# The statistics pass of a two-layer graph network: a sixth selected chunk, one absolute on VectorE, five difference buffers, pair squares one instruction later

## The reference, cut to what matters

```
D = |x[b,i] - x[b,j]|                       for every pair i, j of rows of a batch
h = W1 D + b1                               (64 values per pair)
m, v = mean and variance of h over ALL batches and pairs, per channel
s = W2 . leaky((h - m) / sqrt(v + eps) * g1 + be1) + b2
A = softmax of s over j, where A_init allows the pair
y = A x, a linear layer, batch norm, leaky; out = layernorm(x + [x, y] Wt + bt)
```

## Time and profile before

| what | us |
|---|---|
| median of three runs | 2326.1 (2325.75 to 2334.32) |
| the profiled execution, its own time | 2333.18 |
| its span, first to last instruction | 2330.9 |
| PE (TensorE matmul) busy | 1995.3, 86% |
| DVE (VectorE) busy | 2120.4, 91% |
| ACT (ScalarE) busy | 2165.3, 93% |
| POOL (GpSimd) busy | 43.2, 2% |

### The profile page before, as it was taken

The page is one execution under the profiler, slowest core; times in us unless marked ns, Lnnn a source line. Parts: engine busy times, 40 slices in busy tenths (PEclk is TensorE's granted clock), DMA queues, the critical chain, the costliest instruction groups (busy, mean ns, idle before and its releaser), DMA issues.

```text
span 2330.9 us, 35023 instructions
## 1 busy us (share of the span) xinstructions
PE 1995.3 (86%) x12741; PEld 799.4 (34%) x12741; DVE 2120.4 (91%) x2647; ACT 2165.3 (93%) x2988; POOL 43.2 (2%) x50
## 2 busy tenths in 40 slices
PE   5777777899999898989889899996899999999976
PEld 4555553333333333333333333332222222222226
DVE  5888868999999999999999999998999999999966
ACT  5999987999999999999999999996999999999975
POOL 0000000000000000000000000000000000000000
PEclk8999988999999999999999999998999999999997
DMA  4111104444444444444444444443899989989962
GB/s 122 42 42 42 42 15 149 183 182 180 190 182 181 185 181 184 186 184 177 185 174 185 180 180 190 176 186 156 341 349 354 354 347 357 352 340 354 352 242 73
DMA packets 221280, 470.49 MB, mean 202 GB/s; under 512 B 52344, under 2 KB 143288, under 8 KB 196536
## 3 DMA queue, kind: packets, MB, share of 16 engines
q1 hardware_dynamic: 220048, 467.91, 53.1%
q10 hardware_dynamic: 1064, 0.36, 0.1%
HBM read 254.25 MB, written 213.91 MB: 201 GB/s over the span
## 4 chain that ended last, share of the span: by engine, by line
ACT 42%; issue 23%; PE 13%; DMA 10%; DVE 9%; SPq 4%; ACTq 0%; POOLq 0%; POOL 0%; DVEq 0%
ACT hcopy L625 8%; ACT habs L625 8%; ACT yt L630 8%; ACT diff L613 7%; DMA ring_scores<-sring 4%; DVE ring L1085 4%; ACT habs L657 3%; PE banks L784 3%; PE banks L870 3%; PE banks L955 2%; DMA hcopy<-kept 2%; DMA diff<-kept 2%; ACT banks L635 2%; PE banks L794 2%; SPq L453 2%
## 5 line engine op out<-in xcount | busy, mean ns | idle before, releaser
L870 PE MATMUL banks<-diff,w1t 128*64 128x512 f32 x5136 | 1207.8, 603 | 122.0 <-ACT hcopy L625 57.0
L1213 DVE TENSOR_TENSOR diff<-ring 128x2048 f32<-128x2048 f32 x352 | 802.4, 2287 | 42.1 <-PE banks L870 42.1
L870 PEld LDWEIGHTS banks<-diff,w1t 128*64 128x64 f32 x5136 | 346.7, 137 | 855.3 <-issue 808.3
L1227 DVE TENSOR_SCALAR diff<-diff 128x2048 int32<-128x2048 int32 x354 | 418.2, 1220 | 0.0
L1353 DVE TENSOR_TENSOR diff<-ring 128x2048 f32<-128x2048 f32 x128 | 292.5, 2285 | 17.6 <-PE banks L870 17.4
L613 ACT ACTIVATE diff<-banks 128x2048 f32<-128x2048 f32 x128 | 238.5, 1863 | 2.8 <-PE banks L885 2.8
L955 PE MATMUL banks<-habs,w2s 128*32 128x512 f32 x816 | 159.1, 600 | 55.0 <-ACT hcopy L657 22.4
L630 ACT ACTIVATE yt<-hcopy,par 128x2048 f32<-128x2048 f32 x96 | 192.5, 2005 | 3.1
L630 ACT ACTIVATE yt<-habs,par 128x2048 f32<-128x2048 f32 x96 | 192.4, 2005 | 3.1
L625 ACT ACTIVATE hcopy<-banks 128x1024 f32<-128x1024 f32 x192 | 193.8, 1018 | 0.6 <-PE banks L870 0.6
L625 ACT ACTIVATE habs<-banks 128x1024 f32<-128x1024 f32 x192 | 193.7, 1018 | 0.3 <-PE banks L870 0.3
(11 more groups left out here) (215 smaller groups left out, 1929.0 us busy)
## 6 DMA issues: line engine op xcount, KB each, us to landing
kept<-hcopy SPq DMA_DIRECT2D x192, 512.0 KB, 2.9
kept<-habs SPq DMA_DIRECT2D x192, 512.0 KB, 2.9
hcopy<-kept SPq DMA_DIRECT2D x78, 1024.0 KB, 8.1
diff<-kept SPq DMA_DIRECT2D x76, 1024.0 KB, 8.3
habs<-kept SPq DMA_DIRECT2D x38, 1024.0 KB, 8.4
yt<-xrows SPq DMA_DIRECT2D x512, 40.0 KB, 2.0
adjt<-in_adj_dram SPq DMA_DIRECT2D x32, 256.0 KB, 2.8
diff<-in_x_dram SPq DMA_DIRECT2D x32, 128.0 KB, 2.1
```

What stands on the lines that cost most here:

```text
L870: last = nc.tensor.matmul(dst[half * O:(half + 1) * O, bank * BANK:(bank + 1) * BANK], w1t[:, :], src[:, m * BANK:(m + 1) * BANK], start=T ...
L1213: v.tensor_tensor(shaped(diff[:, c % ND, :]), xj, xi_, ALU.subtract).then_inc(sub_done, 1)
L1227: v.tensor_scalar(bits, bits, ABS_BITS, None, ALU.bitwise_and).then_inc(abs_dve, 1)
```

## The change

Five edits, all in the statistics pass but the last:

1. ORDER is changed, and (1, 1) joins the selected chunks: six of 16 instead of five. They stand at places 0, 3, 6, 8, 11 and 14.
2. The absolute of the selected chunk (0, 1), at place 8, is taken by VectorE out of `dps` (`absolute_of_picked`). ScalarE keeps five: four with a sum, one without, as before. VectorE has ten subtractions and ten absolutes in SBUF, before eleven of each.
3. ND is 5 instead of 4, and `band` gives up two of its three planes for the room. The build of the mask uses `prob` for a while, and GpSimd's masking reads the one plane twice.
4. The square of a pair of copies stands behind the next chunk's `sum_h` in ScalarE's queue and ahead of the absolute, no longer right behind the pair's second copy.
5. VectorE's order is written out anew, to fit.

The blocks of x for the selections grow with the number of selected chunks (NP = 6).

```diff
-    ND = 4
+    ND = 5
-    ORDER = [(0, 0), (4, 0), (4, 1), (1, 0), (5, 0), (5, 1), (2, 0), (6, 0), (6, 1), (3, 0), (7, 0), (7, 1),
-             (0, 1), (1, 1), (2, 1), (3, 1)]
-    ON_PE = [(0, 0), (1, 0), (2, 0), (3, 0), (0, 1)]
+    ORDER = [(0, 0), (4, 0), (4, 1), (1, 0), (5, 0), (5, 1), (2, 0), (2, 1), (0, 1), (6, 0), (6, 1), (3, 0),
+             (7, 0), (7, 1), (1, 1), (3, 1)]
+    ON_PE = [(0, 0), (1, 0), (2, 0), (0, 1), (3, 0), (1, 1)]
+    PE_TO_DVE = [(0, 1)]
...
-        band = sb("band", [P, 3, P])
+        band = sb("band", [P, P])
...
@@ ScalarE
-                    if n % 2:
-                        both = hcopy if n % KB < 4 else habs
-                        src = both[:, n % 4 - 1:n % 4 + 1, :].rearrange("p q n -> p (q n)")
-                        act.wait_ge(kept_copied, n + 1)
-                        nc.scalar.activation(spare, src, ACT.Square, bias=par[:, 53:54],
-                                             accum_out=column(SQUARES + B * NR + n // 2)).then_inc(sq_kept, 1)
...
+            def square_pair(n):
+                both = hcopy if n % KB < 4 else habs
+                src = both[:, n % 4 - 1:n % 4 + 1, :].rearrange("p q n -> p (q n)")
+                act.wait_ge(kept_copied, n + 1)
+                nc.scalar.activation(spare, src, ACT.Square, bias=par[:, 53:54],
+                                     accum_out=column(SQUARES + B * NR + n // 2)).then_inc(sq_kept, 1)
...
                 for j in range(CHUNKS):
                     sum_h(b, j)
-                    if j + 3 in PE_AT:
+                    if pair_ends_at(b, j - 1):
+                        square_pair(b * NK + kept_before(j - 1))
+                    if j == 0 and b:
+                        square_pair(b * NK - 1)
+                    if j + 3 in ACT_AT:
                         absolute(b, j + 3)
...
@@ TensorE, pick_differences
-                if n:
-                    pe.wait_ge(abs_pe, n)
-                e = 2 * pe_before(j)
+                last_pick = [i for i in PE_AT if i < j]
+                if last_pick and last_pick[-1] not in ACT_AT:
+                    pe.wait_ge(abs_dve, b * (CHUNKS - NA) + dve_before(last_pick[-1]) + 1)
+                elif n:
+                    pe.wait_ge(abs_pe, b * NA + act_before(j))
+                k, tp = ORDER[j]
+                e = 2 * (RECTS * tp + k)
...
@@ VectorE
+            def absolute_of_picked(b, j):
+                c = in_order(b, j)
+                dve.wait_ge(pd_ready, b * NP + pe_before(j) + 1)
+                dve.wait_ge(h_ready, c - ND + 1)
+                v.tensor_scalar(diff[:, c % ND, :].bitcast(I32), dps.bitcast(I32), ABS_BITS, None,
+                                ALU.bitwise_and).then_inc(abs_dve, 1)
...
-                    differences_between(b, 1, 3)
-                differences_between(b, 4, 6)
-                differences_between(b, 7, 9)
-                differences_between(b, 10, 12)
+                    subtract(b, 1)
+                    subtract(b, 2)
+                    absolute_at(b, 1)
+                    absolute_at(b, 2)
+                subtract(b, 4)
+                subtract(b, 5)
+                absolute_at(b, 4)
+                subtract(b, 7)
+                absolute_at(b, 5)
+                absolute_at(b, 7)
+                subtract(b, 9)
+                absolute_of_picked(b, 8)
+                subtract(b, 10)
+                absolute_at(b, 9)
+                absolute_at(b, 10)
+                subtract(b, 12)
+                absolute_at(b, 12)
                 subtract(b, 13)
-                subtract(b, 14)
+                subtract(b, 15)
                 absolute_at(b, 13)
-                subtract(b, 15)
-                absolute_at(b, 14)
                 absolute_at(b, 15)
```

More of the change, by code:

```diff
@@ L57, in gnn_pair_kernel @@
     PE_AT = [j for j, c in enumerate(ORDER) if c in ON_PE]
+    ACT_AT = [j for j in PE_AT if ORDER[j] not in PE_TO_DVE]
+    NA = len(ACT_AT)
     STEPS = (0, 4, 1, 5, 2, 6, 3, 7)
@@ L318, in pe_before, with act_before @@
             return sum(a < j for a in PE_AT)
+        def act_before(j):
+            return sum(a < j for a in ACT_AT)
         def dve_before(j):
-            return j - pe_before(j)
+            return j - act_before(j)
         block = ctx.enter_context(nc.Block())
@@ L490, in _ @@
                                     channel_multiplier=-1).then_inc(head_ready, 1)
-            nc.gpsimd.memset(band[:, :, :], 1.0).then_inc(band_one, 1)
-            pool.wait_ge(band_one, 1)
-            nc.gpsimd.affine_select(out=band[:, 0, :], in_=band[:, 0, :], compare_op=ALU.is_ge, fill=0.0, base=-1,
+            far_band = prob[:, 0, 0:P]
+            nc.gpsimd.memset(far_band, 1.0).then_inc(band_one, 1)
+            nc.gpsimd.memset(band[:, :], 1.0).then_inc(band_one, 1)
+            pool.wait_ge(band_one, 2)
+            nc.gpsimd.affine_select(out=band[:, :], in_=band[:, :], compare_op=ALU.is_ge, fill=0.0, base=-1,
                                     pattern=[[1, P]], channel_multiplier=-1)
-            nc.gpsimd.affine_select(out=band[:, 1, :], in_=band[:, 1, :], compare_op=ALU.is_ge, fill=0.0, base=-QUART - 1,
+            nc.gpsimd.affine_select(out=far_band, in_=far_band, compare_op=ALU.is_ge, fill=0.0, base=-QUART - 1,
                                     pattern=[[-1, P]], channel_multiplier=1).then_inc(band_one, 1)
-            pool.wait_ge(band_one, 2)
-            nc.gpsimd.affine_select(out=band[:, 0, :], in_=band[:, 0, :], compare_op=ALU.is_ge, fill=0.0, base=QUART,
+            pool.wait_ge(band_one, 3)
+            nc.gpsimd.affine_select(out=band[:, :], in_=band[:, :], compare_op=ALU.is_ge, fill=0.0, base=QUART,
                                     pattern=[[-1, P]], channel_multiplier=1).then_inc(band_low, 1)
             pool.wait_ge(band_low, 1)
-            nc.gpsimd.tensor_tensor(band[:, 0, :], band[:, 0, :], band[:, 1, :], ALU.add).then_inc(band_low, 1)
-            pool.wait_ge(band_low, 2)
-            nc.gpsimd.tensor_copy(band[:, 2, :], band[:, 0, :]).then_inc(band_ready, 1)
+            nc.gpsimd.tensor_tensor(band[:, :], band[:, :], far_band, ALU.add).then_inc(band_ready, 1)
             nc.gpsimd.memset(ub[:, :, :, :], 0.0).then_inc(ub_zero, 1)
@@ L513, in mask_blocks @@
                 pool.wait_ge(u_loaded[q], 16 * 7 * (b // 2 + 1))
-                nc.gpsimd.tensor_tensor(ub[:, q, 0:3:2, :], ub[:, q, 0:3:2, :], band[:, 0:3:2, :], ALU.mult).then_inc(u_masked, 1)
+                nc.gpsimd.tensor_tensor(ub[:, q, 0:3:2, :], ub[:, q, 0:3:2, :],
+                                        bass.AP(band, 0, [[P, P], [0, 2], [1, P]]), ALU.mult).then_inc(u_masked, 1)
             pool.wait_ge(band_ready, 1)
@@ L636, in sum_h, with pair_ends_at @@
                                          accum_out=column(SQUARES + b * NR + REDONE.index(ORDER[j]))).then_inc(sq_redone, 1)
+            def square_pair(n):
[4 more added lines that the diff above has]
+                                     accum_out=column(SQUARES + B * NR + n // 2)).then_inc(sq_kept, 1)
+            def pair_ends_at(b, j):
+                return j >= 0 and ORDER[j] not in REDONE and (b * NK + kept_before(j)) % 2 == 1
             absolute(0, 0)
@@ L1229, in absolute_at @@
             def absolute_at(b, j):
[L1231 to L1238, removed]
+                absolute(in_order(b, j), b * (CHUNKS - NP) + j - pe_before(j) + 1)
+            def absolute_of_picked(b, j):
[4 more added lines that the diff above has]
+                                ALU.bitwise_and).then_inc(abs_dve, 1)
             half_stat = prob[:, 0, 0:24].rearrange("p (n s) -> p n s", s=6)
             def half_statistics(j):
+                dve.wait_ge(band_ready, 1)
                 dve.wait_ge(h_ready, B * CHUNKS + j + 1)
```

12 lines of the change are left out of this document (6 added, 6 removed).

## The result

The changed kernel takes 2406.91 us (median of four runs, 2405.69 to 2411.39) against 2326.99 (median of four, the three of the table above and one more); the ratio is 1.0339, 95% interval 1.0320 to 1.0358. It is slower by 80 us; 2386 was forecast, with a range of 2362 to 2414.

What follows compares the result with a forecast made beforehand. ScalarE's own work with six 0.15 us self-waits was taken to bound the 38.36 us batch. Median 2326.1 + 48 (31 x 1.6 = 50, less 2 at the pass's end) + 12 for TensorE's clock = 2386 us, range 2362 to 2414.

Steps and rivals of the forecast that it cites:

- What bounds the kernel: Statistics pass: ScalarE's own work, with six 0.15 us waits of pair squares for their copies, is the 38.36 us batch.
- The handshake: ScalarE's takes of projected chunks: c-2 to c needs 3.24 us; 1.24 us idle before takes 3 and 6, 2.5 a batch.
- Rival 3: ScalarE's queue: six self-waits go and three takes in a row cost nothing; 29 us less, 2297 us; chance 0.05.
- rival 4: ScalarE's queue: only one of the two idles shows, the other hidden; 11 us more, 2337 us; chance 0.08.
- VectorE's absolute: VectorE's new absolute out of PSUM: 2.2 us, bounds 1.14 and 4.7; VectorE's batch 35.6 us, its price moving nothing.
- Rival 5: VectorE sets the period after all, its work reaching 40 us through a PSUM absolute of 6.6 us; chance 0.02.
- The clock: TensorE: a 2.5 us gap a batch before projection 3 can lower its clock; 12 us, bounds 0 and 49.
- Rival 1: TensorE's clock never falls in the pass: +48 us, 2374 us; chance 0.25.
- rival 2: TensorE's clock falls at projection 3 in every batch: 48 + 49 us, 2423 us; chance 0.10.
- the two rows that were to show such a fall: Earlier trace, TensorE: after gaps of 2.25 and 2.38 us eight matmuls took 3.68 and 3.47 us, against 1.94 at 2.4 GHz.
- The ends of the pass: Pass's end, where TensorE waits 3 us for two half chunks: 2 us of gain, bounds 0 and 3.
- The fifth buffer: Five difference buffers take away VectorE's four 0.33 us waits a batch for a projection; worth nothing in the steady batch.

Runs made afterwards that it cites:

- E3: The kernel before with only its pair squares moved, spread so that no three takes stand in a row; old order, four buffers: 2301.13 us, ratio 0.9875.
- E1: The changed kernel with only its six pair squares moved in ScalarE's queue so that no three takes stand in a row: 2302.12 us, ratio 0.9879.
- E4: The changed kernel with two more unused products (0.86 us) behind projection 2 in TensorE's queue, cutting its 2.3 us gap in two: 2381.22 us, ratio 1.0215.
- E5: The kernel before with only its pair squares moved one instruction down, as in the change; old order, four buffers, five selections: 2481.42 us, ratio 1.0644.
- E2: The changed kernel with the pair squares back right behind the pair's second copy, all else as changed: 2365.68 us, ratio 1.0151.
- E6: The changed kernel with the absolute of chunk 8 on ScalarE like the other five, VectorE having none out of PSUM: 2411.34 us, ratio 1.0337.
- E7: The changed kernel with four difference buffers instead of five: 2408.49 us, ratio 1.0329.
- E8: The changed kernel with spread pair squares and four difference buffers instead of five: 2335.53 us, ratio 1.0014.

## Why the prediction came out as it did

**What bounds the kernel: right.** ScalarE's queue with its six self-waits was the period. E3 takes nothing away but the self-waits and gets 38.37 - 37.51 = 0.86 us a batch.

**The handshake: right, place and price.** The two holes are before takes 3 and 6, 1.2 us each; the period at full clock is 39.98 us where 39.95 was forecast, and 31 times the difference is the 50 us of the sum. E1, E4 and E5 show it from three sides: no three takes in a row, no hole; holes with the clock held up, 50 us; four such places, four holes. Rival 3 (the handshake costs nothing) and rival 4 (one place hidden) fall with the 58 waits in 29 batches. At the second place the selection of chunk 8 is level with the handshake, as worked out: it starts at 965.60 behind ScalarE's absolute, and projection 6 follows it at 966.70, 1.25 us behind take 4. E5 has no selection there and the same 1.11 us of idle, so the hole doesn't need it.

**VectorE's absolute: right** at 2.21 us against 2.2, and off the path: E1 has it, E3 doesn't, and they take the same time. Rival 5 falls: VectorE is idle 4 us a batch, waiting for projections. The Trainium skill's rule ("VectorE: DVE Perf Modes", Why PSUM operands drop a tier) holds in this trace: the earlier trace rows has 1220 ns on the mean for the same operation in SBUF, and the new one has 2292 ns out of PSUM (32 of them), 1.12 ns a column.

**The clock: the mechanism right, the size too small.** The gap is 2.29 us as the profile counts it (2.5 in starts). The term was 32 x 0.5 x 0.77 = 12 us; it measured 21 x 1.48 = 31. Both factors were too small, the price above all: I halved 1.53 because the slow stretch could fall on covered projections, but in all 21 batches it fell on projection 3, the one nobody covers, which then took 3.09 to 3.63 us. Share and price were guesses between two bounds, and the total is right only within its range: 19 of the 21 us by which 2386 fell short are this term. E4 shows that it is the gap: the same kernel with the gap cut has no long batch. With 31 for 12 the forecast would have been 2405. Rival 1 (never, 2374) and rival 2 (in every batch, 2423) lie on either side.

One of the two rows that were to show such a fall was misread. The gap of 2.25 us in the earlier trace rows ends at 376.36, but the granted clock was 0.50 already at 372.60, before that gap began. The other row holds: the clock was 1.00 in the gap of 2.38 us and 0.50 in the projection behind it (views of the kernel before, as in the earlier trace rows):

```profile
372.60:374.10 1.50, 1.50 (x16) 0.73 (x8) 1.50 (x1) 0.00 (x0) 0.00 (x0) 0.50 1.02 288
1686.30:1688.60 2.30, 0.00 (x0) 0.00 (x0) 2.30 (x3) 2.30 (x3) 0.00 (x0) 1.00 0.34 52
1690.40:1693.40 3.00, 3.00 (x8) 0.69 (x8) 0.20 (x1) 3.00 (x5) 0.00 (x0) 0.50 1.00 423
```

So a single fall stood behind the forecast of this term.

In the kernel of the Trainium skill ("TensorE: Matmul & The Clock Gate", HAM oscillation) each tile's wait is one of some 3 to 5 us for a DMA. The prediction took from it that every batch here would fall; with a gap shorter than those waits that doesn't follow. Two batches in three did so here with the gap of 2.29 us, and none in E2, whose longest wait for a copy is 1.7 us.

**What stays open** is the share. The gap ahead of projection 3 is 2.29 us in the changed kernel, in E5 and in E6, and the batch is long 21, 21 and nine times of 31; in E7 the gap is 2.15 us and the batch long seven times. At full clock the batch is 39.98 us in the changed kernel, 42.42 in E5, 40.52 in E6 and 40.59 in E7, so the share doesn't simply fall as the batch gets longer. It isn't mere chance either: in E6 and E7 the long batches come three to five batches apart, with one exception in E6 (the first two are two apart). No run here tells what sets it.

**The ends of the pass: near.** Two microseconds of gain were taken for the pass's end; start and end together gave 4.

**The fifth buffer: worth nothing to the sum, but not to the new order.** The sum took it at nothing against the kernel before, and the new order has it, so the sum held. That it would be worth nothing in the old order was not run; E3 speaks for it, where ScalarE has no idle time with four. In the new order it isn't a spare part: without it a batch is 0.6 us longer in the changed kernel (E7) and 1.1 us with the squares spread, 33 us in all (E8). Nor did it take VectorE's waits away: they are 4.0 us a batch now, four times 0.33 before, since VectorE has less to do than the period is long.

**A version that beats both.** E1 and E3 are 1.2% faster than before, by 29 and 30 us. What bounds them is ScalarE at 300.00 of 300. E3 is the simpler one: it moves six squares and needs none of the other four edits.

## What to carry to other kernels

When two engines hand work back and forth over two buffers, look at what the slower one's queue holds between taking item c-2 and item c: there must be as much other work in every such interval as the round trip lasts less the takes themselves. Work that waits for nothing (here the pair squares) is filler, and is worth most where it splits a run of takes; moving it to save 0.15 us cost 1.23 us in each interval that it left empty. Write the queue out in order before moving an instruction, count three-in-a-rows, and look at what a filler's leaving does to the other engine's clock.

## What was not expected of the hardware

Adding four matmul instructions a batch to TensorE made the kernel 26 us faster by its median (E4, 2381.22 against 2406.91), through the granted clock alone: the holes are as they were, and every batch is as long as the changed kernel's batches at full clock.

The means of ScalarE's groups grew although nothing got slower: the copy of L632 lasts 1056 ns on the mean after, 1018 before, yet copies still start 1.00 us apart (944.77 and 943.77 in the earlier trace rows, 958.18 and 957.18 after). In the rows above, copies last 1.11 and 1.12 us ahead of the first hole and 1.02 and 1.03 behind it. So a row's length there holds something beside the instruction's own work; what, no run shows. Distances between starts are the price, row lengths are not.
